# More unread 512-column products on TensorE: in the linear groups of steps 9 to 11, in steps 12 to 14 and between the last softmaxes and projections

## The reference, cut to what matters

```python
h = patches @ proj_w.T + proj_b                       # 1152 x 192
a = layernorm(h)
q, k, v = split(fake_quant(a) @ fake_quant(ww1).T)    # 12 heads of 64
dots = fake_quant(q) @ fake_quant(k).T * scale        # per image: 36 x 36 per head
out = fake_quant(softmax(dots)) @ fake_quant(v)
h = h + fake_quant(out) @ fake_quant(ww2).T + bb2
x = layernorm(h)
top = argmax(x @ Wg + bg)                             # one of 4 experts per token
h = h + (gelu(x @ W1[top] + b1[top]) @ W2[top] + b2[top])
```

## Time and profile before

| | |
|---|---|
| median of 3 runs | 176.65 us (176.25 to 178.95) |
| the profiled execution | 176.16 us, its span 174.4 us |
| mean granted TensorE clock | 0.873 of full speed |
| busy: PE, DVE, ACT, POOL | 139.1, 129.9, 119.8, 41.7 us |
| share of the chain that ended last | PE 41%, DVE 22%, issue 12%, DMA 11%, ACT 5% |

### The profile page before, as it was taken

How to read it: one execution, slowest core, us unless ns; L and a number is a source line. 1 busy time by engine, 2 the same in 40 slices (tenths; PEclk the granted TensorE clock), 3 DMA queues, 4 the chain that set the end, 5 groups by cost and what they waited for, 6 DMA issues and landing times.

```text
span 174.4 us, 5210 instructions
## 1 busy us (share of the span) xinstructions
PE 139.1 (80%) x1845; PEld 110.4 (63%) x1845; DVE 129.9 (74%) x395; ACT 119.8 (69%) x232; POOL 41.7 (24%) x104
## 2 busy tenths in 40 slices
PE   0498799995599879997869876643799999999960
PEld 0498777852355546664557656531279999999950
DVE  2628847999998998999999876759535766767650
ACT  8934477499679968999999763540087778778710
POOL 7214543240000010101011015656000422332242
PEclk9999999999656969999996558555899999999996
DMA  3799999999999998000000001234595010001000
GB/s 85 293 323 291 348 349 223 241 248 371 368 371 371 365 373 349 17 0 4 4 0 4 0 8 53 106 145 157 162 304 197 26 33 26 26 12 49 4 26 24
DMA packets 12922, 27.72 MB, mean 159 GB/s; under 512 B 1745, under 2 KB 8667, under 8 KB 12897
## 3 DMA queue, kind: packets, MB, share of 16 engines
q1 hardware_dynamic: 11744, 24.41, 43.6%
q0 software_dynamic: 1152, 2.97, 4.7%
HBM read 15.39 MB, written 12.29 MB: 159 GB/s over the span
## 4 chain that ended last, share of the span: by engine, by line
PE 41%; DVE 22%; issue 12%; DMA 11%; ACT 5%; SPq 4%; POOL 3%; POOLq 0%; DVEq 0%; ACTq 0%
PE lin_bank L1337 12%; DMA patches<-in_patches 8%; PE head_bank L1075 3%; PE head_bank L1349 3%; PE lin_bank L1108 3%; PE head_bank L1357 3%; PE head_bank L1350 3%; PE lin_bank L1104 2%; DVE mx L733 2%; DVE w L728 2%; DVE dif L739 2%; DVE aint L852 2%; DMA slots<-row,slot 2%; DVE den L844 2%; DVE aq L661 2%
## 5 line engine op out<-in xcount | busy, mean ns | idle before, releaser
L622 ACT ACTIVATE q<-lin_bank,b 128x128 f32<-128x128 f32 x72 | 25.0, 369 | 7.3 <-PE lin_bank L1337 6.6
L1337 PE MATMUL lin_bank<-q,w 128*128 128x128 f16 x360 | 29.6, 219 | 0.3 <-ACT q L612 0.3
L1337 PEld LDWEIGHTS lin_bank<-q,w 128*128 x360 | 23.7, 98 | 0.8 <-issue 0.6
L1075 PE MATMUL head_bank<-proj_w,patches 128*128 128x192 f32 x84 | 16.9, 359 | 7.3 <-DMA patches<-in_patches 7.3
L446 POOL DMA_INDIRECT out<-q,patches x12 | 11.8, 987 | 38.0 <-DVE q L1038 37.7
L1046 DVE CAST q<-q 128x384 f16<-128x384 f32 x24 | 8.6, 360 | 16.1 <-ACT q L622 16.1
L1075 PEld LDWEIGHTS head_bank<-proj_w,patches 128*128 128x128 f32 x84 | 15.5, 213 | 7.5 <-issue 6.7
L1108 PE MATMUL lin_bank<-xqT,ww1q 96*128 96x288 bf16 x96 | 16.2, 297 | 3.1 <-ACT vint L483 2.3
L419 POOL TENSOR_TENSOR rstd<-veps,nhalf 128x1 f32<-128x1 f32 x7 | 3.9, 554 | 60.7 <-DVE veps L679 60.7
L1349 PE MATMUL head_bank<-early,q 128*128 x72 | 17.7, 246 | 0.3 <-DVE q L1051 0.3
L1357 PE MATMUL head_bank<-early,q 128*128 x72 | 17.7, 246 | 0.0
(11 more groups left out here) (141 smaller groups left out, 342.0 us busy)
## 6 DMA issues: line engine op xcount, KB each, us to landing
slots<-blank SPq DMA_DIRECT2D x3, 2938.0 KB, 21.2
patches<-in_patches SPq DMA_DIRECT2D x9, 384.0 KB, 11.1
patches<-slots SPq DMA_DIRECT2D x12, 226.0 KB, 4.3
patches<-in_w SPq DMA_DIRECT2D x4, 576.0 KB, 12.4
early<-in_ww SPq DMA_DIRECT2D x3, 576.0 KB, 10.6
patches<-in_w SPq DMA_DIRECT2D x4, 384.0 KB, 11.6
patches<-in_w SPq DMA_DIRECT2D x8, 192.0 KB, 13.3
proj_w<-in_proj_w SPq DMA_DIRECT2D x1, 576.0 KB, 4.4
```

The lines of the kernel that those rows point to most:

```text
L622: a.activation(g[:, j % 2, m], up_bank[n % 4][:, 0:P], ACT.Gelu, scale=1.0 / WSCALE, bias=b1[:, bass.ds(e, 1), m]).then_inc(g_ok, 1)
L1075: last = mm(emb_bank[t][:, 0:E], patches[:, t, kc], proj_w[:, kc], start=kc == 0, stop=kc == KE - 1)
L1337: last = mm(up_bank[n % 4][:, 0:P], up_weights(j, part, m), xT[:, j % 3, piece], start=x == 0, stop=x == len(PASSES) - 1)
```

## The change

`KEEP_TO` goes from 9 to 12, so that the three linear groups of step 9, the two of step 10 and the two of step 11 get one unread product each. In each of the steps 12, 13 and 14 a first three unread products stand ahead of the projection, behind a wait for the evacuation of the last linear group, and a second three behind `attend`; all go to `lin_bank[0][:, 0]`. In the tail ten go to `score_bank`: two before `probs_T(14)`, behind a wait for the last read of the scores, three before `probs_T(15)`, two before `attend(14)`, three behind `count(0)`. No result is read from any of the 35, and no other instruction is added, removed or moved.

```diff
-    KEEP_FROM, KEEP_TO = 2, 9
+    KEEP_FROM, KEEP_TO = 2, 12
...
+            def keep(bank, n):
+
+                for x in range(n):
+                    mm(bank, ones[:], ww2q[:].rearrange("p m n -> p (m n)")[:, 0:512], start=True, stop=True)
+
...
+                if i >= KEEP_TO:
+                    pe.wait_ge(lin_int, len(lin_order))
+                    keep(lin_bank[0][:, 0], 3)
                 for t in tiles_at(i, 0):
                     if i < STEPS - 1:
                         project(t)
                 if i >= 2:
                     attend(i - 2)
+                if i >= KEEP_TO:
+                    keep(lin_bank[0][:, 0], 3)
...
             attend(13)
             norm_T(4)
+            pe.wait_ge(dif_ok, PAIRS)
+            keep(score_bank[:], 2)
             probs_T(14)
             project(5)
+            keep(score_bank[:], 3)
             probs_T(15)
+            keep(score_bank[:], 2)
             attend(14)
             attend(15)
             count(0)
+            keep(score_bank[:], 3)
             pe.wait_ge(xnT_ok, 5)
             project(6)
             project(7)
```

## The result

The changed kernel took 177.37 us (median of 12 runs) where the kernel before took 176.45 (12 runs beside it); the ratio is 1.0081, with a 95% interval of 1.0041 to 1.0121. Within 2% it is the same; inside those it is slower, by 0.7 to 2.1 us. The ratio compares the means of the executions that kept to the chip's faster state, 10 of the 12 of the changed kernel and 8 of the 12 of the kernel before, so it isn't the quotient of the two medians. Run again beside the kernel before on another occasion, it came to 1.0044 (1.0012 to 1.0077). The profiled execution took 177.36 us, span 175.6, against 176.16 and 174.4. So + 1.2 us from one profiled execution to the other, where + 0.7 was forecast. The forecast of 177.3 for the median is met, in part by luck: it stood on a median of 176.65 before, which 12 runs made 176.45, and from median to median the change is + 0.92.

A forecast was written before the change was run, and what follows sets the result against it. The chain was taken as mostly VectorE's waits to about 96.6 us, then TensorE's work from 97.19 to 104.69. A residual + 0.69 later made 176.16 into 176.85, plus 0.49 for the median 177.3; range 174.4 to 179.2.

The forecast's parts named there:

- The mechanism: Step 12 through the tail: TensorE keeps full clock, but products overrun its idle time; + 0.69 us in sum.
- idle ahead of step 12's products: Step 12: TensorE waits 0.26 us, from 89.22 to 89.48, for ScalarE's delayed last linear evacuation.
- scores of step 14: After step 13, taken as 2.65 us at full clock: these scores start at 96.04.
- end of the gate of step 14: Step 14: the gate ends at 98.88 where it ended at 98.15, making VectorE 0.73 us late.
- `attend(15)`: Tail: it starts at 103.60, its result at 103.97 against 103.28, 0.69 us late.
- residual of `project(6)`: End of the tail: VectorE's residual starts at 105.38 where it started at 104.69, 0.69 us late.
- The term that was mis-sized: Steps 12 to 14 and tail: each unread product costs TensorE 0.22 us at full clock, start to start.
- The tail: Behind step 14: a delay of 0.73 us ends as 0.69, 0.15 given back by the clock, last three products just covered.
- Steps 9 to 11: Seven products, 1.5 us of TensorE, delay ScalarE by 0.44; felt only at the new wait in step 12.
- the products vanish in waits: Rival, chance 0.20: all 28 later products fit beside other engines, leaving the clock's gain of 2.2 us; 173.9, median 174.4.
- ScalarE's delay is carried on: Rival, chance 0.10: late exponentials delay VectorE up to 0.44 in each of steps 12 to 14; 178.2, median 178.7.
- the clock falls all the same: Rival, chance 0.06: clock falls at 92.67, 22 products cost 0.42 each; + 9.0 us, 185.2, median 185.7.

The follow-up runs named there:

- e2_steps: Against the kernel before: only the 18 unread products of steps 12 to 14, none in steps 9 to 11 or the tail; ratio to before 1.0006.
- e7_earlier: The changed kernel, with the wait ahead of the products of steps 12 to 14 one evacuation earlier; ratio to the kernel before 1.005.
- e4_narrow: The changed kernel, with the 28 products of steps 12 to 14 and the tail cut from 512 to 64 columns; ratio to the kernel before 0.9987.
- e12_sparse: The version with 15 products less seven: five in steps 12 to 14, three in the tail; ratio to the kernel before 1.0061.
- e3_tail: Against the kernel before: only the ten products of the tail, none in steps 9 to 14; ratio to the kernel before 1.0132.
- e11_cov_linear: The version with 15 products plus the seven products of steps 9 to 11; ratio to the kernel before 0.998.

## Why the prediction was right

**The mechanism, right.** The clock stayed full from 92.7 through the tail, as forecast, and its gain was spent on products that TensorE had no idle time for. The product counts (0.215 us for each one more) and the version with fewer products show it. Step by step, from the scores of step 12:

| point | forecast | measured |
|---|---|---|
| idle ahead of step 12's products | 0.26 | 0.16 |
| scores of step 13 | 4.59 | 4.53 |
| scores of step 14 | 7.24 | 7.24 |
| end of the gate of step 14 | 10.08 | 10.36 |
| `attend(15)` | 14.80 | 15.20 |
| residual of `project(6)` | 16.58 | 16.99 |

**The size, short by 0.4.** Of the + 1.10 on the stage, + 0.69 were forecast. The term that was mis-sized is the product followed by a group that isn't a linear group. I took 0.22 from a product ahead of its linear group; three products took 0.75 ahead of `probs_T` (91.15 to 91.90, and 97.73 to 98.48), 0.72 and 0.73 ahead of `attend` (93.56 to 94.70 and 96.27 to 97.42, less 0.42 for the scores), and the two ahead of `attend(14)` 0.53 (102.50 to 103.03) where 0.44 was taken. Only ahead of `norm_T` and of the projection was it 0.66. That is 0.40 in all. The gate of step 14 took 0.61, where 0.51 had been read the earlier trace rows: 0.10 more.

Two terms went the other way. The wait in step 12 was 0.16 and not 0.26: from ScalarE's end to the first product it took 0.05 (89.55 to 89.60), where the 0.14 ahead of `attend(15)` had been taken. And the gates of step 12 took 1.36 and not 1.41. That the scores of step 14 start at 7.24 as forecast, to the hundredth, is luck: there the products were 0.15 longer, and these two terms took it back. What is left of the 0.41 are hundredths in the starts of the groups.

**The tail, right in kind.** Products and clock nearly cancel there: 6.42 before, 6.50 after, 6.06 with the clock and no products (e2_steps).

**Steps 9 to 11, right.** The seven products of steps 9 to 11 were given no cost but the wait in step 12; 15.18 and 15.19 us say so, and e7_earlier puts the wait at 0.16.

**The rivals.** That the products vanish in waits was wrong of this kernel. In the kernel with 15 they did vanish, but the stage gave 0.9 of the 2.2 us that I had priced, as VectorE's pace takes over (busy 8.87 of 8.90). That ScalarE's delay is carried on was half right. The sign that I named for it, VectorE waiting for an exponential in steps 12 to 14, did come, once (0.2) and not in each step, and in the changed kernel it cost nothing; in the kernel with 15 products and the seven it cost 0.3. That the clock falls all the same didn't happen in the two profiles of the changed kernel. The rule on idle gaps, from the Trainium skill ("TensorE: Matmul & The Clock Gate", section "Why this matters for your kernels"), would have had the unread products do nothing to the clock; the trace disagrees again: they closed gaps of 0.6 us at most, and the clock stayed. e4_narrow, with the gaps filled by narrow matmuls, lost it.

**What I had not seen** is that the place at which the clock falls, in the kernel before, is not fixed, and moves the stage by 0.5. The forecast was made against one execution with a late fall, and so was the + 1.10 that it is measured by. The other side of the comparison is firmer: the kernel that holds the clock repeats its stage within 0.01 us.

## What to carry to other kernels

Unread matmuls that hold the clock were worth it here only in time in which TensorE would otherwise wait at full clock: list its waits as they will be once the clock is up, and fill those. Beyond that each cost its start distance on the path, here 0.22 to 0.25 us, and 28 of them took more than the clock gave back. To find what such a change does, read a stage between two landmarks on the path beside the span: the version with 15 products repeated its stage within 0.01 us in two executions whose spans differ by 1.2. But the verdict is the time's over many runs. The clock can fall at another place in the stage (0.5 us here) or once more behind it, and the shorter stage of e12_sparse came with longer runs.

## What the runs showed of the hardware that I had not expected

The same code, up to the tail, lost its clock 3.9 us behind the scores of step 12 in one execution (before, at 92.67) and 2.8 us behind them in another (e3_tail, at 90.9), and the twelve gate matmuls took 1.54 or 2.53 us by it. Where the clock was held through the stage, its length did not move: the stage of the changed kernel was 16.99 and 16.98 in two executions, that of the version with 15 products 14.98 and 14.99. That version is near an edge: with seven products added far ahead of it, in steps 9 to 11, the clock fell in its tail (e11_cov_linear), where it had held twice without them; whether it holds in every execution isn't shown by three profiles. And of the same kernel with 15 products one execution lost the clock again at 126.5, at the start of the experts, and the other did not.
